# Three dense feed-forward parts of a four-layer network: another order of the filling work, earlier begun units, and every second output product of the third part in split FP32R terms

## What is computed

```python
def _L2_ffn_ref(x, gate_w, gate_b, w1, b1, w2, b2, ws1, bs1, ws2, bs2):
    xf = x.reshape(-1, DIM)                        # 2048 tokens, DIM 128
    logits = xf @ gate_w + gate_b                  # 8 experts
    top_w, top_i = jax.lax.top_k(logits, K)        # K = 2
    gw = jax.nn.softmax(top_w, axis=-1)
    combine = (gw[:, :, None] * jax.nn.one_hot(top_i, E)).sum(1)
    out = jnp.zeros_like(xf)
    for e in range(E):
        h = jax.nn.gelu(xf @ w1[e] + b1[e])        # hidden size 512
        out = out + combine[:, e:e+1] * (h @ w2[e] + b2[e])
    shared = jax.nn.gelu(xf @ ws1 + bs1) @ ws2 + bs2
    return out + shared
```

## Time and profile before

| | us |
|---|---|
| median of 3 runs | 3156.63 |
| lowest and highest | 3143.51, 3161.05 |
| the profiled execution, its own time | 3160.24 |
| its span, from the first to the last instruction | 3158.4 |
| TensorE busy in the span | 88% |
| VectorE, ScalarE, GpSimd busy | 52%, 37%, 37% |
| mean granted clock of TensorE, share of full speed | 0.916 |

### The profile page before, as it was taken

One profiled execution on the slowest core, in us unless ns is written; L12 is line 12 of the kernel. 1 busy time (PEld: TensorE's weight loads), 2 busy tenths in 40 slices (PEclk: granted clock), 3 DMA queues, 4 the chain that ended last, 5 costly groups with the idle time before them and its releaser, 6 DMA issues. The chain is left out here.

```text
span 3158.4 us, 39502 instructions
## 1 busy us (share of the span) xinstructions
PE 2763.7 (88%) x15392; PEld 1562.1 (49%) x15392; DVE 1644.6 (52%) x3016; ACT 1162.8 (37%) x2373; POOL 1160.3 (37%) x1101
## 2 busy tenths in 40 slices
PE   6999998889979998577788888899978999997889
PEld 3444454656644444245556556556533333334556
DVE  3444444523347761158677778412256766765623
ACT  1233232322316670032155556234433334332422
POOL 2322311165531100047454444058713443442255
PEclk8899998899979997889888999799979999998999
DMA  2000001021100002026322222211000000001032
GB/s 91 1 1 1 1 1 70 1 68 40 54 38 1 1 1 85 14 69 167 97 69 71 61 58 55 93 41 54 14 0 1 1 0 1 1 1 45 1 122 107
DMA packets 32605, 126.25 MB, mean 40 GB/s; under 512 B 9249, under 2 KB 12066, under 8 KB 25858
## 3 DMA queue, kind: packets, MB, share of 16 engines
q1 hardware_dynamic: 30882, 120.58, 11.7%
q0 software_dynamic: 1536, 3.15, 0.4%
HBM read 105.82 MB, written 16.78 MB: 39 GB/s over the span
## 5 line engine op out<-in xcount | busy, mean ns | idle before, releaser
L306 PE MATMUL ps<-parts 128*128 128x512 f32 (+7 forms) x5400 | 1210.6, 439 | 89.1 <-DVE fw_sb L336 39.4
L306 PEld LDWEIGHTS ps<-parts 128*128 128x128 f32 (+3 forms) x5400 | 651.7, 191 | 621.2 <-issue 338.3
L316 ACT ACTIVATE work<-ps 128x512 f32<-128x512 f32 (+6 forms) x898 | 487.1, 569 | 878.9 <-PE ps L306 772.4
L320 POOL TENSOR_TENSOR work<-work 128x512 f32<-128x512 f32 (+1 forms) x404 | 500.7, 1241 | 609.7 <-ACT work L316 389.4
L336 DVE TENSOR_REDUCE fw_sb<-ps 128x2 f32<-128x1024 f32 (+3 forms) x384 | 415.1, 1086 | 276.8 <-PE ps L306 275.7
L306 PE MATMUL ps<-work,fw_sb 128*128 128x512 f32 (+1 forms) x832 | 383.9, 557 | 18.0 <-POOL work L320 15.7
L306 PE MATMUL ps<-work 128*32 128x256 f32 (+5 forms) x2396 | 366.7, 422 | 35.7 <-DMA work<-work 27.3
L316 ACT ACTIVATE fw_sb<-ps 128x512 f32<-128x512 f32 (+5 forms) x394 | 204.6, 536 | 314.1 <-PE ps L306 271.7
L320 DVE TENSOR_TENSOR work<-work,ps 128x512 f32<-128x512 f32 (+1 forms) x204 | 127.0, 622 | 275.0 <-POOL work L320 270.5
L310 PE MATMUL ps<-wc_sb,fw_sb 128*128 128x128 f32 x1128 | 208.1, 298 | 36.5 <-DVE work L357 11.7
L306 PEld LDWEIGHTS ps<-work 128*32 128x32 f32 (+2 forms) x2396 | 139.9, 138 | 196.1 <-issue 133.4
(11 more groups left out here) (142 smaller groups left out, 3142.5 us busy)
## 6 DMA issues: line engine op xcount, KB each, us to landing
work<-scr_w SPq DMA_DIRECT2D x32, 1024.0 KB, 4.7
work<-scr_places SPq DMA_DIRECT2D x64, 256.0 KB, 3.9
work<-scr_sk SPq DMA_DIRECT2D x64, 128.0 KB, 2.6
scr_sp<-wr_sb SPq DMA_DIRECT2D x64, 128.0 KB, 2.2
fw_sb<-in_f SPq DMA_DIRECT2D x1, 6528.0 KB, 18.0
fw_sb<-in_f SPq DMA_DIRECT2D x1, 5376.0 KB, 15.6
fw_sb<-in_f SPq DMA_DIRECT2D x1, 4608.0 KB, 17.9
work<-scr_w SPq DMA_DIRECT2D x8, 512.0 KB, 6.4
```

The source lines that it names most:

```text
L306: return self.e.matmul(o, l, r, start=start, stop=stop) if self.e else Unwritten()
L316: return self.e.activation(o, i, f, bias=bias, scale=scale)
L320: return self.e.tensor_tensor(o, a, b, op) if self.e else Unwritten()
```

## The change

- `rows` is now one step per chunk (`row_pe`, `row_dve`), and the four stand between consecutive fill items from `rows_at` on; `rows_at` goes from 8 to 7 (layer 0), 10 to 9 (layer 2), 12 to 10 (layer 3).
- `ahead`, the expert units in the fill, goes from 2 to 3 (layer 0) and 1 to 2 (layer 3). Up to four `weigh` items are taken at each step of main, not one, and the downs behind them are no longer capped at two a step. The ring `F` grows from 10 to 14 and from 7 to 11 entries, and the buffer of the turned rows moves into `W`'s second buffer to make room.
- SyncE waits for the landing of group 0's load before it issues group 1's, in all three.
- Layer 2 gets `split` = 3: for chunks 1 and 3 of each unit the hidden values are split too (a new step `parts` one pair after `up`: ScalarE copies the high part, VectorE subtracts), and `down` of those pairs is `three`, three FP32R matmuls, in place of one FP32 product. `down` runs three pairs behind `up`. The split of a unit's weights covers 256 columns, not 128, and since the down product reads it too, the wait ahead of `part` is now for the former unit's last `down`.

The diff, cut to its core (of the two `parts` steps the first is ScalarE's, the second VectorE's):

```diff
-        for c in range(NC):
-            e.wait_ge(*k.summed[t, "rows", c])
-            e.copy(self.wT[0:E, ch(c)], self.Mb[1][0:E, :]).then_inc(*k.made_v.up((t, "rows", c)))
+        e.wait_ge(*k.summed[t, "rows", c])
+        e.copy(self.wT[0:E, ch(c)], self.Mb[1][0:E, :]).then_inc(*k.made_v.up((t, "rows", c)))
...
-        self.H = A.parting(3, 256 * (self.w - 1))
+        self.m = 128 * (self.w if split else self.w - 1)
+        self.split = split
+        self.H, self.A = A.parting(3, 2 * self.m), A.parting(split, 1024)
...
+        self.parted = [uc for uc in main if split and uc[1] % 2]
+        for uc in self.parted:
+            self.A.take(uc)
...
-            if i == rows_at:
-                self.order.append(("rows", 0, 0))
+            if 0 <= i - rows_at < NC:
+                self.order.append(("rows", 0, i - rows_at))
...
             if c == 1 and n.index(u) + 2 < len(n):
                 self.order.append(("part", n[n.index(u) + 2], 0))
-            if first:
-                self.order.append(("weigh", *first[0]))
+            for uc in first[:4]:
+                self.order.append(("weigh", *uc))
                 pend.append(first.pop(0))
             self.order.append(("up", u, c))
+            if i and main[i - 1] in self.parted:
+                self.order.append(("parts", *main[i - 1]))
             pend.append((u, c))
-            m = 2
-            while len(pend) > 2 and m:
+            while len(pend) > (3 if split else 2):
                 self.order.append(("down", *pend.pop(0)))
-                m -= 1
...
+        if uc in self.parted:
+            a = self.A[uc]
+            e.wait_ge(*k.made_v[t, "parts", uc])
+            self.three(e, k.ps[c][:, :], u, self.w - 1, a[:, 0:512], a[:, 512:1024], first, last
+                       ).then_inc(*k.summed.up((t, "down", u, c)))
+            return
...
                 if self.H.before[u] is not None:
-                    e.wait_ge(*k.summed[t, "up" if self.gated else "gate", self.H.before[u], NC - 1])
+                    e.wait_ge(*k.summed[t, "down" if self.split else "up" if self.gated else "gate", self.H.before[u], NC - 1])
...
+            elif what == "parts":
+                a = self.A[u, c]
+                e.wait_ge(*(k.made_v[t, "product", (u, c)] if self.gated else k.made_g[t, "weighed", (u, c)]))
+                if self.A.before[u, c] is not None:
+                    e.wait_ge(*k.summed[(t, "down") + self.A.before[u, c]])
+                e.activation(R(a[:, 0:512]), (self.F if self.gated else self.S)[u, c], ACT.Copy).then_inc(*k.made_a.up((t, "parts", (u, c))))
...
+            elif what == "parts":
+                a = self.A[uc]
+                e.wait_ge(*k.made_a[t, "parts", uc])
+                e.tt(R(a[:, 512:1024]), (self.F if self.gated else self.S)[uc], a[:, 0:512], ALU.subtract
+                     ).then_inc(*k.made_v.up((t, "parts", uc)))
...
         for g, rows in enumerate(self.groups):
+            if g == 1:
+                e.wait_ge(*self.spread[0][0])
...
-        return before + [Experts(k, 0, A, r, hT, 10, units, [], 2, 8, ACT.Silu, True)]
+        return before + [Experts(k, 0, A, r, hT, 14, units, [], 3, 7, ACT.Silu, True)]
-        return before + [Experts(k, 2, A, Routing2(k, A, k.lnT), k.lnT, 0, units, range(32, 36), 0, 10, ACT.Gelu, False, "b1")]
+        return before + [Experts(k, 2, A, Routing2(k, A, k.lnT), k.lnT, 0, units, range(32, 36), 0, 9, ACT.Gelu, False, "b1", 3)]
-    return before + [Experts(k, 3, A, Routing3(k, A, k.lnT), k.lnT, 7, units, range(16, 18), 1, 12, ACT.Silu, True)]
+    return before + [Experts(k, 3, A, Routing3(k, A, k.lnT), k.lnT, 11, units, range(16, 18), 2, 10, ACT.Silu, True)]
```

More of the change, by code:

```diff
@@ L3041, in logits_dve, with row_dve @@
         self.choose_dve(e)
-    def rows_dve(self, e):
+    def row_dve(self, e, c):
         k, t, E = self.k, self.tag, self.E
-        for c in range(NC):
-            e.wait_ge(*k.summed[t, "rows", c])
-            e.copy(self.wT[0:E, ch(c)], self.Mb[1][0:E, :]).then_inc(*k.made_v.up((t, "rows", c)))
+        e.wait_ge(*k.summed[t, "rows", c])
+        e.copy(self.wT[0:E, ch(c)], self.Mb[1][0:E, :]).then_inc(*k.made_v.up((t, "rows", c)))
     def exp_act(self, e):
@@ L3088, in __init__ @@
     def __init__(self, k, A, x):
-        super().__init__(k, "route0", 0, A, x, 8, A.get(T, 8))
         self.W = A.ring(2, T)
+        super().__init__(k, "route0", 0, A, x, 8, self.W.items[1])
         self.t1, self.t2 = self.W.items[0][:, 0:1024], self.W.items[0][:, 1024:2048]
@@ L3193, in __init__ @@
     def __init__(self, k, A, x):
-        super().__init__(k, "route3", 3, A, x, 16, A.get(T, 16))
         self.W = A.ring(2, T)
+        super().__init__(k, "route3", 3, A, x, 16, self.W.items[1])
         self.s, self.gs, self.gq, self.pm = A.get(256), A.get(64), A.get(64), A.get(64)
@@ L3237, with __init__ @@
 class Experts(Stage):
-    def __init__(self, k, l, A, route, x, hidden, units, shared, ahead, rows_at, fn, gated, bias=None):
+    def __init__(self, k, l, A, route, x, hidden, units, shared, ahead, rows_at, fn, gated, bias=None, split=0):
         super().__init__(f"experts{l}")
@@ L3283, in __init__ @@
         self.order += [("down", *uc) for uc in pend]
-        if rows_at >= len(fill):
-            self.order.append(("rows", 0, 0))
         first, pend = [uc for uc in fill if uc[0] not in self.shared], []
@@ L3290, in __init__ @@
                 self.order.append(("part", n[n.index(u) + 2], 0))
-            if first:
-                self.order.append(("weigh", *first[0]))
+            for uc in first[:4]:
+                self.order.append(("weigh", *uc))
                 pend.append(first.pop(0))
             self.order.append(("up", u, c))
+            if i and main[i - 1] in self.parted:
+                self.order.append(("parts", *main[i - 1]))
             pend.append((u, c))
-            m = 2
-            while len(pend) > 2 and m:
+            while len(pend) > (3 if split else 2):
                 self.order.append(("down", *pend.pop(0)))
-                m -= 1
+        if main[-1] in self.parted:
+            self.order.append(("parts", *main[-1]))
         self.order += [("down", *uc) for uc in pend]
@@ L3312, in weights, with three @@
         return self.k.fw[:, (u * self.w + i) * 128:(u * self.w + i) * 128 + 128]
-    def three(self, e, o, u, i, c):
-        h, n = self.H[u], 128 * (self.w - 1)
+    def three(self, e, o, u, i, hi, lo, start=True, stop=True):
+        h, n = self.H[u], self.m
         wh, wl = R(h[:, i * 128:i * 128 + 128]), R(h[:, n + i * 128:n + i * 128 + 128])
[L3317 to L3320, removed]
+        e.matmul(o, wh, R(hi), start=start, stop=False)
+        e.matmul(o, wh, R(lo), start=False, stop=False)
+        return e.matmul(o, wl, R(hi), start=False, stop=stop)
     def logits_pe(self, e):
@@ L3332, in logits_pe, with row_pe @@
         ins.then_inc(*k.summed.up((r.tag, "logits", 0)))
-    def rows_pe(self, e):
+    def row_pe(self, e, c):
         k, r = self.k, self.route
@@ L3337, in rows_pe @@
         e.wait_ge(*k.made_v[r.tag, "weights"])
[L3338 to L3342, removed]
+        e.wait_ge(*k.made_v[r.tag, "rows", c - 1])
+        for i in range(4):
+            ins = e.transpose(r.Mb[1][0:E, tile(i)], r.w[:, (4 * c + i) * E:(4 * c + i) * E + E], k.cst("id"))
+        ins.then_inc(*k.summed.up((r.tag, "rows", c)))
     def fill_pe(self, e, u, c):
@@ L3358, in up_pe @@
         e.wait_ge(*k.made_a[t, "hidden", self.G.before[uc]])
-        self.three(e, self.G[uc][:, :], u, 0, c).then_inc(*k.summed.up((t, "gate", u, c)))
+        self.three(e, self.G[uc][:, :], u, 0, self.xh[:, ch(c)], self.xl[:, ch(c)]).then_inc(*k.summed.up((t, "gate", u, c)))
         if self.gated:
@@ L3365, in up_pe @@
                 e.wait_ge(*k.made_v[self.route.tag, "rows", NC - 1])
-            self.three(e, self.U[uc][:, :], u, 1, c).then_inc(*k.summed.up((t, "up", u, c)))
+            self.three(e, self.U[uc][:, :], u, 1, self.xh[:, ch(c)], self.xl[:, ch(c)]).then_inc(*k.summed.up((t, "up", u, c)))
     def down_pe(self, e, u, c):
@@ L3370, in down_pe @@
         uc = (u, c)
+        first, last = u == self.downs[0][0], u == self.downs[-1][0]
+        if uc in self.parted:
[4 more added lines that the diff above has]
+            return
         if not self.gated:
@@ L3378, in down_pe @@
             e.wait_ge(*k.made_v[t, "product", uc])
-        first, last = u == self.downs[0][0], u == self.downs[-1][0]
         e.matmul(k.ps[c][:, :], self.weights(u, self.w - 1), (self.F if self.gated else self.S)[uc], start=first, stop=last
@@ L3388, in pe @@
             elif what == "rows":
-                self.rows_pe(e)
+                self.row_pe(e, c)
             elif what == "fill":
@@ L3427, in act @@
             e.activation(R(self.xh[:, ch(c)]), self.x[:, ch(c)], ACT.Copy).then_inc(*k.made_a.up((t, "upper", c)))
-        m = 128 * (self.w - 1)
+        m = self.m
         for what, u, c in self.order:
```

(4 more changed lines are left out.)

## The result

The changed kernel takes 3234.58 us (median of 4 executions, 3232.84 to 3236.36), against 3154.20 for the kernel before in the same series: a ratio of 1.0244, 95% interval [1.0219, 1.0270]. It is slower, as forecast, but by 80 us where some 45 were forecast; 3203 was predicted, with a range to 3250. The profiled execution took 3236.36.

The account below looks back on a forecast made before the run. TensorE, busy every microsecond of layer 2's main stretch, was taken as the bound. 3160.24 + 55.7 - 4 - 3.3 - 3.0 = 3205.6 us profiled, 3202 on the median, given as 3203; range 3186 to 3250.

Parts of the forecast that it names:

- The moved wait: Layer 2: `part` on ScalarE waits for the former unit's last down, holding queued work; main stretch +55.7 us.
- the ring: Layer 2 main: dependency loop through all engines, once for each of 29 units; closes at 8.13 us, TensorE idling 2.2.
- The walk: Layer 2: link-by-link timing from the awaited down through ScalarE, GpSimd, VectorE and TensorE, giving 8.13 us a unit.
- The clock: Layer 2: TensorE's clock after each 2.2 us hole; nothing added, up to 50 us in all if slow stretches follow each.
- rival C: Layer 2: clock falls in the ring, slow matmuls after half to all holes, +25 to +50 us, 3228 to 3253; chance 0.26.
- The upper row: Layer 3's attention: a 4.0 us stretch reads clock 0.57; such a stretch behind a hole loses 1.7 us.
- Rival A's arithmetic: Layer 2: wait harmless, GpSimd with VectorE bounds at 3.02 us for two pairs; 3142 on the median; chance 0.07.
- the split product: Layer 2: 64 of 128 pairs change an FP32 down for three FP32R matmuls, -9.8 us if nothing else is late.
- the whole-instruction rule: VectorE with two SBUF inputs and GpSimd reading SBUF exclude each other for the whole instruction; rival A's sum then 3.15.
- Layer 2's turnings: Layer 2's fill: fill items cover waits for VectorE's copies, about 3.3 saved, plus 0.7 of a slow fill item: -4 us.
- Layer 0: Layer 0's stage: earlier weighing and more fill shorten TensorE's idle from 7.14 to 4.5 us; -3.3 us with a slow restart.
- Layer 3: Layer 3's stage: old hole closed, new stall of 5.0 us for expert 2's load; -3.0 us, from -6 to +1.

Follow-up runs that it names:

- The two versions without the ring: Changed kernel with four buffers H in layer 2: 3143.21 us, ratio 0.9960; changed kernel with layer 2's `part` at chunk 3 instead of 1: 3145.92 us, ratio 0.9959.

## Why the prediction was right, and where it was short

**The moved wait** was right, link for link: it closed the ring that was walked, 29 times. The walk gave 8.13 us for a ring; the kernel shows 8.1 where the clock holds, 8.15 with the hole filled, and TensorE idles 1.97 where 2.2 was said. The two versions without the ring, and the wait without the split (6.58 against 6.5), close it from both sides.

**The clock** is the term that was mis-sized. I took nothing for it, as layer 1's experts keep 1.00 with TensorE busy 3.78 of 5 us, and put a chance of 0.26 on rival C with 1.7 us for a ring. It came out as C, nearly in full: 20 of 28 rings paid 1.6 us, 32 of the 35 us by which the main stretch exceeded its forecast; filling the hole took 30.8 us off the stage. The upper row was the nearer one, and the choice between two rows so far apart rested on nothing but a likeness of the matmuls. The two rows differ in how the idle time is cut: layer 1's holes there are of 0.8 to 1.1 us, one in each 3.6 to 3.9 us, this one is 2 us in one piece. The runs have four cases: the clock fell, in 20 of 28 turns, with 1.97 us in each, and not with 0.18, nor with layer 1's, nor with the 1.3 to 1.4 us of the split in every chunk. That points to the length of the piece, but the last case has another mix of matmuls and a turn of 7.48 us, and nothing between 1.4 and 1.97 was run, so the reason for the fall stays argued. One stretch of the trace after, from the FP32 down behind the restart at 2081.71 on, reads (columns as in the earlier trace rows):

```profile
2083.20:2087.10 3.90, 3.90 (x10) 2.40 (x9) 1.09 (x1) 0.27 (x1) 0.84 (x1) 0.56 0.02 4
```

3.90 us at 0.56, near the lower of the two clock levels (1.2 and 2.4 GHz), loses 3.90 x 0.44 = 1.7. The Trainium skill, in "TensorE: Matmul & The Clock Gate", section "HAM oscillation — how this bites in real kernels", describes a matmul kernel whose clock falls anew in every turn of a loop, at a wait for a DMA of some 3 to 5 us. The trace agrees on the fall in turns of a loop, in 20 of 28; it differs in the length, as here a piece of 1.97 us was enough. I had not weighed that section.

**Rival A's arithmetic** (3.02 us for two pairs, from GpSimd and VectorE excluding each other) was not what decided here. Once the ring is gone, 3.03 is measured, but not out of the terms of the sum: four weighings take 5.68 of a unit's 6.07 us, 2.84 for two pairs, and GpSimd waits another 0.39 in each unit for ScalarE. That the sum comes out is in part luck. That the shared path alone sets the pace is not shown; that two pairs take 3.03 and not 2.95 is, and it is why the split product brings less than its 9.8 us. By the whole-instruction rule that the prediction took from the Trainium skill ("SBUF — State Buffer", section "Who interferes with whom") its sum was 3.15; the measured 3.03 lies under it, and a subtraction of 512 columns held by a weighing ends 0.55 us after it (0.54 in the walk), not the 0.69 that it takes alone.

**Layer 2's turnings**: -5.1 against -4. The four turnings saved 3.3 as walked, and the slow item behind them 1.0 where I took 0.7. Another 0.9 I had not counted: the kernel before had a second stretch of slow clock at the end of this stage, from 2077.84 on, and its last eight matmuls there took 4.6 us, against 3.8 after.

**Layer 0**: -3.0 against -3.3, by errors against each other, so the agreement is luck. The last copy ended at 643.53, 1.2 sooner than I had it, and the load landed at 650.8, but that did not help: I had GpSimd weigh from t0 = 652.1 and overlooked its own queue, 12 products instead of 8, then four sums, until 653.2. TensorE restarted at 654.49, later than the 653.80 before, and its hole was 6.49 us where I had 4.5. As group 1 had landed by then, the 1.4 us that I gave to its load did not come; they came, as 1.95, when the sums were moved away.

**Layer 3**: -4.2 against -3.0, with the spread of 4 us that this stage has over the runs. The old hole closed to 0.97 us, the new one was 4.78 where 5.0 was walked. Behind it I had put 2.5 us of slow clock; the four downs there, with their waits for GpSimd, took 4.8 us (3100.10 to 3104.93) where the walk has 3.95, so 0.9.

## What to carry to other kernels

When a wait changes its object, look for the place in the signalling engine's order where the new object stands, and then for what is queued behind the wait on the waiting engine: the same wait two steps later was free here, and where it stood it closed a ring through four engines. A ring is priced by walking it once with rows and comparing it with the bottleneck engine's own work for that turn; only the excess counts: 10 us for the short chain, 60 for the long one at full clock (263.1 - 203.5). On top of it comes the clock: a hole of about 2 us in one piece in every turn deserves to be priced with the slow clock as the likeliest case (holes of 1.4 us did not bring it down here), and filling it with idle matmuls shows the clock's share in one run.

## What the runs showed of the hardware beyond what I expected

- TensorE's clock fell in 20 of 28 turns of a loop in which it was idle for 1.97 us of 8.1 in one piece, and in none when that piece was filled down to 0.18 us, nor in 29 turns of about 7.5 us with an idle piece of 1.3 to 1.4 (the split in every chunk); the 8 turns at full clock came singly, each after one to three slow ones.
- Two engines' instructions that wait for each other's read path both lengthen in the records: with four buffers `H`, weighings from 1.28 to 1.44 us on average, and subtractions of 512 columns from 0.69, as they take with GpSimd idle, to 1.17.
